# Four subtractions per slice of the first layer norm on VectorE instead of GpSimd, for four of eight slices

## The reference, cut to what matters

```
x = x + tanh(g_xattn) * attention(layernorm(x), ctx, ctx, Wq, Wk, Wv, Wd)    # causal, within 64 rows
x = x + tanh(g_ffn) * down(silu(gate(layernorm(x))) * up(layernorm(x)))
#   gate, up, down: linear, with weights w * (su @ sv), su @ sv of rank 4
```

## Time and profile before

| | us |
|---|---|
| median of 3 runs | 1373.98 (1373.82 to 1374.1) |
| the profiled execution | 1372.32 |
| its span in the trace | 1370.5 |
| TensorE busy | 1356.4 |
| VectorE busy | 974.3 |
| GpSimd busy | 953.6 |
| ScalarE busy | 561.9 |

### The profile page before, as it was taken

One profiled execution on the slowest core, in us unless ns is written; L12 is line 12 of the kernel. 1 busy time (PEld: TensorE's weight loads), 2 busy tenths in 40 slices (PEclk: granted clock), 3 DMA queues, 4 the chain that ended last, 5 costly groups with the idle time before them and its releaser, 6 DMA issues.

```text
span 1370.5 us, 21420 instructions
## 1 busy us (share of the span) xinstructions
PE 1356.4 (99%) x7770; PEld 1112.5 (81%) x7770; DVE 974.3 (71%) x1465; ACT 561.9 (41%) x950; POOL 953.6 (70%) x883
## 2 busy tenths in 40 slices
PE   8999999999999999999999999999999999999998
PEld 8988788888888878787777878778888888888887
DVE  6388678786555676666767877774788888766776
ACT  5455655545344432232323333333344434333333
POOL 5599999999788946454545666563787787666664
PEclk9999999999999999999999999999999999999999
DMA  8386787877978866443545556620322331311121
GB/s 293 123 264 219 239 264 246 265 247 247 341 255 288 295 228 226 143 156 127 166 155 161 171 169 190 195 77 25 78 62 63 92 83 47 123 54 47 47 70 70
DMA packets 158057, 226.47 MB, mean 165 GB/s; under 512 B 43264, under 2 KB 89600, under 8 KB 155904
## 3 DMA queue, kind: packets, MB, share of 16 engines
q1 hardware_dynamic: 157952, 225.09, 51.0%
HBM read 155.32 MB, written 69.73 MB: 164 GB/s over the span
## 4 chain that ended last, share of the span: by engine, by line
PE 92%; DVE 3%; POOL 3%; issue 1%; ACT 1%; DMA 0%; DVEq 0%; SPq 0%; ACTq 0%; POOLq 0%
PE bank L616 74%; PE bank L766 4%; PE bank L742 3%; PE bank L888 3%; PE bank L889 3%; PE bank L890 3%; PE bank L659 1%; POOL wa_lo L1674 1%; DVE x_lo L1432 1%; DVE X L1477 1%; DVE bn L1254 0%; DVE xc L1274 0%; POOL ws L1662 0%; PE bank L650 0%; ACT x_hi L1087 0%
## 5 line engine op out<-in xcount | busy, mean ns | idle before, releaser
L616 PE MATMUL bank<-xc,wa_hi 128*128 128x512 f32 x896 | 277.3, 391 | 0.0
L616 PE MATMUL bank<-wd_hi,o_hi 128*128 128x512 f32 x512 | 202.9, 396 | 1.4 <-issue 1.4
L616 PE MATMUL bank<-wd_lo,o_hi 128*128 128x512 f32 x512 | 199.5, 390 | 0.0
L616 PE MATMUL bank<-wd_hi,o_lo 128*128 128x512 f32 x512 | 199.2, 389 | 0.0
L616 PEld LDWEIGHTS bank<-xc,wa_hi 128*128 128x128 f32 x896 | 167.7, 188 | 35.9 <-issue 0.4
L616 PE MATMUL bank<-xc,wa_lo 128*128 128x512 f32 x448 | 174.5, 389 | 0.0
L1063 ACT ACTIVATE o_hi<-bank 128x512 fp32r<-128x512 f32 x128 | 69.6, 596 | 227.4 <-PE bank L766 150.2
L616 PE MATMUL bank<-x_hi,wf_hi 128*128 128x512 f32 x392 | 153.0, 390 | 1.8 <-DVE ft L1442 1.7
L1477 DVE SCALAR_TENSOR_TENSOR X<-bank,tg,X 128x512 f32<-128x512 f32 x221 | 154.4, 741 | 0.0
L616 PE MATMUL bank<-x_hi,wf_lo 128*128 128x512 f32 x392 | 152.5, 389 | 0.0
L616 PE MATMUL bank<-x_lo,wf_hi 128*128 128x512 f32 x364 | 141.7, 389 | 0.0
(11 more groups left out here) (175 smaller groups left out, 3176.2 us busy)
## 6 DMA issues: line engine op xcount, KB each, us to landing
q_scratch<-q_st SPq DMA_DIRECT2D x32, 1024.0 KB, 4.3
q_sb<-q_scratch SPq DMA_DIRECT2D x64, 512.0 KB, 5.0
w_raw<-in_wq SPq DMA_DIRECT2D x32, 512.0 KB, 4.2
wd_raw<-in_wd SPq DMA_DIRECT2D x16, 1024.0 KB, 4.9
f_raw<-ffn_eff_scratch SPq DMA_DIRECT2D x28, 512.0 KB, 3.6
er_raw<-in_sf_r SPq DMA_DIRECT2D x42, 256.0 KB, 3.9
e_raw<-in_wf SPq DMA_DIRECT2D x42, 256.0 KB, 5.4
ffn_eff_scratch<-e_eff SPq DMA_DIRECT2D x42, 256.0 KB, 5.1
```

Of the source, the lines that this page charges most:

```text
L616: last = pe.matmul(to, a, b, start=(start and n == 0), stop=(stop and n == 3 * len(pairs) - 1), skip_group_check=onto)
```

## The change

The four subtractions of slices 0 to 3 move from GpSimd's queue to VectorE's. There they stand at the end of quads 2, 5, 7 and 9, behind `effective` and `lr_lo` of the quad and ahead of the next quad's t1. They signal a semaphore of their own, v_xs, for which ScalarE's `x_hi` waits. GpSimd keeps slices 4 to 7; its counts of g_t start at zero for slice 4. Operands, sizes and order of the subtractions are the same.

```diff
         def x_hi(m):
-            a.wait_ge(g_t, 4 * (m + 1))
+            a.wait_ge(v_xs if m < 4 else g_t, 4 * (m % 4 + 1))
...
+        def x_sums(m):                                             # VectorE
+            v.wait_ge(a_xt, 2 * m + 2)
+            v.tensor_tensor(xb[:, 4], xb[:, 0], xb[:, 1], ALU.subtract).then_inc(v_xs, 1)
+            v.tensor_tensor(xb[:, 6], xb[:, 3], xb[:, 0], ALU.subtract).then_inc(v_xs, 1)
+            v.wait_ge(v_xs, 4 * m + 1)
+            v.tensor_tensor(xb[:, 5], xb[:, 3], xb[:, 4], ALU.subtract).then_inc(v_xs, 1)
+            v.wait_ge(v_xs, 4 * m + 3)
+            v.tensor_tensor(xb[:, 7], xb[:, 5], xb[:, 2], ALU.subtract).then_inc(v_xs, 1)
...
             if q + 1 in E_AT:
                 lr_lo(E_AT[q + 1])
+            if q in COLUMNS and COLUMNS[q] < 4:
+                x_sums(COLUMNS[q])
             if q in STATS and q in X_SPLIT:
                 stats1(STATS[q])
...
-            g.wait_ge(g_t, 4 * m + 1)                              # GpSimd's x_sums
+            g.wait_ge(g_t, 4 * (m - 4) + 1)
...
-            g.wait_ge(g_t, 4 * m + 3)
+            g.wait_ge(g_t, 4 * (m - 4) + 3)
...
-            if q in COLUMNS:                                       # GpSimd's quad
+            if q in COLUMNS and COLUMNS[q] >= 4:
                 x_sums(COLUMNS[q])
```

More of the change, by code:

```diff
@@ L195, in flamingo @@
     v_c1 = sem("v_c1")
-    g_t, g_s, g_wa, g_wd, g_xn = sem("g_t"), sem("g_s"), sem("g_wa"), sem("g_wd"), sem("g_xn")
+    v_xs, g_t, g_s, g_wa, g_wd, g_xn = sem("v_xs"), sem("g_t"), sem("g_s"), sem("g_wa"), sem("g_wd"), sem("g_xn")
     g_t2, g_fs, g_fw, g_dn, g_c22 = sem("g_t2"), sem("g_fs"), sem("g_fw"), sem("g_dn"), sem("g_c22")
```

## The result

The changed kernel takes 1379.99 us (median of 6 runs, 1378.65 to 1382.36) against 1373.46 us for the kernel before in the same series: 6.5 us more, ratio 1.0049, interval 1.0038 to 1.0060. Measured again with the experiments it is 1379.12 against 1374.62: 4.5 us more, ratio 1.0034 (1.0022 to 1.0047). All intervals are 95%. I had forecast slower, 1377.6 us, with 1374.8 to 1379.8 as range. The direction and the places of the two large stalls were right; the size was too small.

What follows compares the result with a forecast made beforehand. The prediction took TensorE, busy 99% of the span, to bound the kernel. Its steps summed as 1.6 - 0.6 + 0 + 0.7 + 0 - 1.0 + 2.9 = +3.6 us, giving 1377.6 us, range 1374.8 to 1379.8.

Steps and rivals of the forecast that it cites:

- The price of the four: VectorE's four moved subtractions: 1.4 us alone, 3.05 beside GpSimd's 256-wide ones, up to 5.5 with a 1024-wide partner.
- Steps 1, 3 and 6: TensorE later: quad 3 for t1, +1.6 us; quad 8 start behind ScalarE's copy, +0.7; quad 10 for t1, +2.9.
- only short partners: Rival: the 1024-wide GpSimd instruction misses quad 10, 0.6 us there, sum +1.3, 1375.3 us; chance 0.14.
- Step 2: Quad 4: with TensorE 1.6 us later, most of its old gap for t1 is filled, -0.6 us.
- Step 4: Quad 8: idle time and slack before t1 cover x_sums(2), 0 us (0 to 1.1).
- Step 5: Before quad 10: GpSimd's chain to ScalarE's copy ends about where it did, so TensorE's gap is filled, -1.0 us.
- After quad 10 nothing can give it back: After quad 10: no TensorE wait is left in the projections, so the +3.6 us stays.
- Long partners all over: Rival: every place meets a 512- or 1024-wide GpSimd instruction and the gaps stay, about +7 us, 1381 us; chance 0.07.
- Relief: Rival: the four take 1.4 us everywhere within the slacks, GpSimd's 3 us fill quads 4 and 10: 0 to -1.7 us; chance 0.17.

Runs made afterwards that it cites:

- psum_operand: The changed kernel, but each of VectorE's four subtractions takes one operand from PSUM: 1372.83 us, ratio 0.9990 to the kernel before.
- slice2_psum: The changed kernel, but only the four subtractions of slice 2 (end of quad 7) take an operand from PSUM: 1377.87 us, ratio 1.0030 to the kernel before.
- stall_longer: The kernel before with thirteen unused statistics of s1 on VectorE ahead of t1 in quad 10: 1380.79 us, ratio 1.0049.
- left_out: The subtractions of slices 0 to 3 done on neither engine, results not the kernel's: 1371.26 us, ratio 0.9975 to the kernel before.
- r_after: The changed kernel unedited, run again for a second profile: 1379.12 us, ratio 1.0034 to the kernel before.
- only_slice3: The change for slice 3 alone (end of quad 9), slices 0 to 2 staying on GpSimd: 1376.61 us, ratio 1.0024 to the kernel before.

## Why the prediction was right or wrong

- *The price of the four.* Right. 3.05 us forecast for quad 3, 3.06 measured; 1.4 and 1.6 for quad 6; up to 5.5 and 5.4 for quad 8; 5.45 and 5.1 for quad 10. psum_operand shows that the price above 1.4 us is the second SBUF operand.
- *Steps 1, 3 and 6.* Right: 1.6, 0.7 and 2.9 forecast, 1.61, 0.47 and 2.94 measured. x_sums(3) met the 1024-wide partner as worked out, but two us later than forecast, 163.09 in place of 161.1: both queues were late together. That the size of this stall fits is in part luck. In slice2_psum the meeting was missed and the stall was 3.42 us, since er paid for it; the rival "only short partners" had 0.6 us there.
- *Step 2.* Half right: -0.6 forecast, -0.3 measured.
- *Step 4.* 0 forecast, 0.4 measured, within its bound of 1.1. Of the four, two met a long partner.
- *Step 5 failed.* It took the gap before quad 10 as filled, -1.0, on the argument that the chain through GpSimd "ends about where it did". The copy stood at 155.99 and stands at 158.32: it moved with TensorE. I had given x_sums(2) a length of up to 5.5 us but counted it against t1 alone; behind t1 stand the statistics. Their last result, veps, for which GpSimd's power waits, came at 146.06 in place of 140.79, 3.5 us later relative to TensorE, and GpSimd, which had been relieved of 2.9 us, stood 2.64 us for it. It began the power 2.3 us later than before (146.31, 144.00), and the copy is later by the same 2.3. slice2_psum shows it: with that one group at 1.5 us the gap and the stall of quad 8 are gone. The step is 1.0 us of the miss. VectorE's veps and GpSimd's power before, then veps in the changed kernel:
```profile
140.79 0.23 DVE L1263 TENSOR_SCALAR veps<-moments 128x2 f32<-128x2 f32 x1
...
144.00 0.71 POOL L1631 TENSOR_TENSOR rstd<-veps,neg_half 128x2 f32<-128x2 f32 x1
```
```profile
146.06 0.17 DVE L1263 TENSOR_SCALAR veps<-moments 128x2 f32<-128x2 f32 x1
```
- *"After quad 10 nothing can give it back"* was right, but I took it to mean that nothing is lost there either. After the stall come 1.5 to 2.2 us more in the two profiles, at half clock in one, as gaps in quads 17, 21 and 30 in the other. stall_longer shows both without any moved work. This term was missing from the sum altogether.
- The sum by quad 10: 3.6 forecast, 1.6 - 0.3 + 0.5 + 0.4 + 0 + 2.9 = 5.1 measured in gaps, 5.6 in the shift of line 659's matmul. 1.5 us of the difference are steps 2, 4 and 5. With what came later the shift is 7.8 us in one profile and 7.0 in the other, more than the 6.5 and 4.5 of the medians. So the two profiles show which terms the prediction had wrong; how much of the miss in the medians each carries is not settled, and the two series differ by 2 us themselves.
- *Rivals.* "Long partners all over" came nearest in time, 1381, by other terms: the long partners were in quads 8 and 10 only. "Relief" is what psum_operand shows once the turns are taken away, and left_out more than it: 3.4 us where I had put the ceiling of any gain at 1.7.
- Not settled: why left_out gains 3.4 us when its profile shows 1.1; what makes the late gaps; and what decides whether a stall of 2.9 us is followed by half clock. It was in two of the three profiles with 2.94 or 2.95 us (r_after, only_slice3), not in the third, not in those with 2.65 and 3.42, and it was after 5.08.

## What to carry to other kernels

Before moving a short operation from GpSimd to VectorE, count its SBUF inputs: with two, it cost in these runs the rest of whatever GpSimd subtraction was running, once for each instruction, and what it delays is everything behind it in the queue, also what sends GpSimd its next work. If one operand still stands in PSUM, read it there. And a stall of a saturated TensorE may cost more than its length: check the granted clock of the stretch behind it. The medians show it only weakly here: +3.0 and +3.3 us for stalls of 2.65 and 2.95, +6.9 (5.1 to 8.4) for 5.08.

## What the runs showed of the hardware that I had not expected

- A 128x256 float32 subtraction on VectorE with one operand in PSUM takes 408 to 425 ns, alone or beside GpSimd subtractions 256 to 1024 wide (psum_operand); with both in SBUF 418 to 2510 ns (the changed kernel).
- After stalls of 2.95 us TensorE's clock was 1.2 GHz in place of 2.4 for 3.4 us (r_after, only_slice3); with one of 5.08 us it was so for 6.8 us, from 1.7 us before the stall's end (stall_longer). Two executions of one kernel with the same stall, 2.94 and 2.95 us, differed in this.
